# Two bursts of whole expert tiles in each of the last six iterations of the token pipeline, instead of all 71 tiles behind it

## What is computed

```python
x = x + conv_ref(group_norm(x), ...)      # depthwise 3x3, input-dependent weights, plus residual
t = tokens(x)
t = t + attn_ref(layer_norm(t), ...)      # hash buckets -> 32 pooled keys and values per image,
                                          # 8 heads of attention, then a GELU MLP 64 -> 256 -> 64
t = t + ffn_ref(layer_norm(t), ...)       # mixture of experts
# ffn_ref, for each token n, with 8 experts of hidden size 682 and the two likeliest chosen:
logits = flat @ router_w.T
topk_probs, topk_idx = top_k(softmax(logits), 2)
gates  = topk_probs / (sum(topk_probs) + 1e-9)
out[n] = sum over k of gates[k] * (silu(flat @ w1[e_k].T) * (flat @ w3[e_k].T)) @ w2[e_k].T
```

## Time and profile before

| | |
|---|---|
| median of 3 runs | 801.96 us (799.52 to 803.97) |
| profiled execution, its own time | 802.19 us |
| its span in the trace | 800.40 us |
| PE busy | 650.6 us, 81% of the span |
| DVE busy | 463.2 us, 58% |
| ACT busy | 353.7 us, 44% |
| POOL busy | 371.8 us, 46% |
| HBM read and written | 58.54 and 16.47 MB |

### The profile page before, as it was taken

The page is one execution under the profiler, slowest core; times in us unless marked ns, Lnnn a source line. Parts: engine busy times, 40 slices in busy tenths (PEclk is TensorE's granted clock), DMA queues, the critical chain, the costliest instruction groups (busy, mean ns, idle before and its releaser), DMA issues.

```text
span 800.4 us, 13968 instructions
## 1 busy us (share of the span) xinstructions
PE 650.6 (81%) x4632; PEld 487.2 (61%) x4632; DVE 463.2 (58%) x1094; ACT 353.7 (44%) x693; POOL 371.8 (46%) x377
## 2 busy tenths in 40 slices
PE   2597989797979797866206999999999999999960
PEld 2475858585857576664104777677777777777740
DVE  2356677686868676643502566655555665555545
ACT  1143646373727273533203555455555445555520
POOL 2204241767676768727670343334444333444440
PEclk9667868797978788575656999999999999999995
DMA  2000000010101010101173455555556455554608
GB/s 85 0 14 1 14 1 14 19 49 17 51 18 38 18 38 17 51 5 53 50 182 86 148 161 160 165 161 162 179 161 167 152 168 168 179 156 150 191 8 314
DMA packets 46615, 75.47 MB, mean 94 GB/s; under 512 B 7488, under 2 KB 30048, under 8 KB 46544
## 3 DMA queue, kind: packets, MB, share of 16 engines
q1 hardware_dynamic: 34512, 57.12, 24.5%
q0 software_dynamic: 8640, 12.74, 4.8%
q10 hardware_dynamic: 3392, 4.73, 1.8%
HBM read 58.54 MB, written 16.47 MB: 94 GB/s over the span
## 4 chain that ended last, share of the span: by engine, by line
PE 49%; POOL 23%; issue 17%; DVE 6%; DMA 3%; ACT 1%; POOLq 0%; SPq 0%; ACTq 0%; DVEq 0%
PE bk L757 25%; POOL expert_rows L497 15%; PE bk L768 12%; PE bk L745 3%; POOL rr L452 3%; PE bk L775 2%; POOL r L463 1%; PE bk L554 1%; POOL r L458 1%; POOL x2t L481 1%; DMA out<-hid 1%; DMA srow<-expert_results 1%; PE bk L642 1%; POOL grstd L441 1%; PE bk L616 1%
## 5 line engine op out<-in xcount | busy, mean ns | idle before, releaser
L1266 DVE TENSOR_TENSOR units<-bk,silu 128x512 f32<-128x512 f32 x213 | 147.3, 692 | 165.7 <-ACT silu L943 165.7
L519 POOL DMA_INDIRECT expert_results<-yout,xin x142 | 139.5, 983 | 218.3 <-DVE yout L1277 191.5
L757 PE MATMUL bk<-xs,wbuf 64*128 64x256 f32 x1704 | 205.5, 388 | 1.1 <-ACT xs L930 1.1
L757 PEld LDWEIGHTS bk<-xs,wbuf 64*128 64x128 f32 x1704 | 160.8, 189 | 44.4 <-issue 26.6
L943 ACT ACTIVATE silu<-bk 128x512 f32<-128x512 f32 x213 | 127.2, 597 | 87.2 <-PE bk L757 87.2
L497 POOL DMA_INDIRECT expert_rows<-srow,pos x128 | 132.4, 1034 | 44.2 <-issue 37.9
L768 PE MATMUL bk<-units,wbuf 128*64 128x256 f32 x852 | 107.6, 388 | 0.0
L768 PEld LDWEIGHTS bk<-units,wbuf 128*64 128x64 f32 x852 | 54.8, 136 | 32.4 <-issue 11.7
L935 ACT ACTIVATE ysb<-bk 128x256 f32<-128x256 f32 x71 | 27.2, 383 | 84.3 <-PE bk L768 84.3
L452 POOL TENSOR_TENSOR rr<-vare,c_mhalf 128x16 f32<-128x16 f32 x8 | 23.4, 2923 | 74.6 <-DVE vare L1046 74.6
L745 PE MATMUL bk<-const,xin 128*128 128x128 f32 x142 | 31.3, 302 | 29.2 <-DMA xin<-expert_rows 29.2
(11 more groups left out here) (184 smaller groups left out, 963.2 us busy)
## 6 DMA issues: line engine op xcount, KB each, us to landing
wbuf<-in_weights SPq DMA_DIRECT2D x71, 576.0 KB, 4.1
xin<-expert_rows SPq DMA_DIRECT2D x71, 130.0 KB, 2.4
expert_results<-yout,xin POOLq DMA_INDIRECT x142, 2.8
xg<-in_x SPq DMA_DIRECT2D x8, 256.0 KB, 2.8
expert_rows<-srow,pos POOLq DMA_INDIRECT x128, 2.4
srow<-expert_results SPq DMA_DIRECT2D x8, 256.0 KB, 5.1
srow<-expert_results ACTq DMA_DIRECT2D x8, 256.0 KB, 5.9
out<-hid ACTq DMA_DIRECT2D x8, 256.0 KB, 5.2
```

What stands on the lines that cost most here:

```text
L519: g.indirect_dma_start(results[:, :], bass.IndirectOffsetOnAxis(ap=xin[:, t % X_SLOTS, h, ROW - 1:ROW].bitcast(U32), axis=0), yout[:, t % ...
L757: last = mm(bank[:, ch * MT:(ch + 1) * MT], wbuf[part, t % W_SLOTS, at:at + P], xs[part, t % 2, :], start=True, stop=True)
L1266: tt(units[:, t % 2, q, :], h3_ps[q], silu[:, q, :], ALU.mult).then_inc(unit_ready, 1)
```

## The change

Iterations 0 to 4 (`ramp`) keep their lists. Iterations 5 to 10 (`mix`) have a new list on every engine, and in each of them PE runs two bursts of whole tiles, one ahead of the attention scores and one behind `fc2`. There is no iteration 11: the sixteen scatters of a group now all go out within its stage d. Because a tile may only take rows that are already scattered, tiles belong to rounds: iteration 5 has nine tiles, 6 to 9 have eight each, and iteration 10 has two in its first burst and the remaining 28 in its second. A tile of an early round must be full, which is known once the groups before have been counted; `schedule`, on DVE, works out each round's experts and rows from running counts. The router's product is now four matmuls with both halves of the tokens at once instead of eight, and the shifted scores and the probabilities (`ssub`, `prob`) have four buffers instead of two.

```diff
-ROW_SLOTS = 3
+ROW_SLOTS = 2
...
+MIX = 5
+FIRST_ROUND = 1
+ROUND_TILES = [0, 9, 8, 8, 8, 8, 8]
+MIXED = sum(ROUND_TILES)
...
+        def y_bank(t):
+            return (bk7, bk0)[(BURST_END[t] - 1 - t) % 2]
...
+def bursts():
+
+    table = {}
+    t = 0
+    for i in range(MIX, NG + 3):
+        n = ROUND_TILES[i - MIX + FIRST_ROUND]
+        half = 2 if i == NG + 2 else n // 2
+        last = i == NG + 2
+        table[i, 0] = (t, t + half)
+        table[i, 1] = (t + half, NT if last else t + n)
+        t += n
+    return table
```

SP loads three tiles ahead, weights and rows together (before: rows up to six ahead); the first rows of a round wait for that round's last scatter:

```diff
+            def load_tile(t):
+                if t < NT:
+                    load_weights(t)
+                    if t == MIXED:
+                        write_pads()
+                    load_rows(t)
+
+            def burst(i, part):
+                for t in range(*BURSTS[i, part]):
+                    load_tile(t + W_SLOTS - 1)
```

On POOL, the second burst has the scatters of rows and of results between each other:

```diff
+                run(d, row_destinations)
+                run(d, scatter, 0, 5)
+                if last:
+                    run(d, scatter, 5, 11)
+                else:
+                    run(c, rstd3)
...
+                if i == MIX:
+                    run(c, residual)
+                    run(d, rstd3)
+                    run(c, rstd2)
+                run(a, group_rstd)
...
+                def in_second(k):
+                    if k == 0:
+                        run(a, token_rstd)
+                        run(c, rstd3)
+                    if k == 1:
+                        run(b, rstd2)
+                    if i < NG + 2:
+                        run(d, scatter, 8 + 2 * k, 2 if k < 4 else 0)
+                    if k == 3:
+                        run(b, residual)
+                        run(a, token_sum)
+                        run(a, unit_sum)
+
+                burst(i, 0, in_first)
+                run(d, row_destinations)
+                run(d, scatter, 0, 8 if i < NG + 2 else 16)
+                burst(i, 1, in_second)
```

On PE:

```diff
+            def mixed_iteration(i, a=None, b=None, c=None, d=None):
+                if i == MIX:
+                    run(c, attend, 2)
+                    run(c, attend, 3)
+                    run(d, turn_wtok)
+                else:
+                    run(d, turn_wtok)
+                    turn_results(BURSTS[i - 1, 1][1] - 1)
+                    run(b, turn_n1, 0)
+                run(b, turn_n1, 1)
+                run(d, router)
+                run(b, rotate)
+                run(a, pair_means)
+                run(b, queries, 0)
+                run(c, turn_n2)
+                run(b, queries, 1)
+                run(a, pair_variances)
+                run(b, bucket_sums)
+                run(b, turn_pooled)
+                run(b, keys)
+                run(b, values)
+                turn_rows(BURSTS[i, 0][0])
+                burst(i, 0)
+                run(b, scores, 0)
+                turn_results(BURSTS[i, 0][1] - 1)
+                run(b, scores, 1)
+                run(a, convolution, 0)
+                run(b, scores, 2)
+                run(a, convolution, 1)
+                run(b, scores, 3)
+                run(d, places)
+                run(b, turn_prob, 0)
+                run(b, turn_prob, 1)
+                run(c, fc1, 0)
+                run(b, attend, 0)
+                run(b, attend, 1)
+                run(b, turn_prob, 2)
+                run(b, turn_prob, 3)
+                run(c, fc1, 1)
+                run(b, attend, 2)
+                run(b, attend, 3)
+                turn_rows(BURSTS[i, 1][0])
+                run(c, fc2)
+                burst(i, 1)
```

On ACT, what lies between the tiles of a burst (k is the tile's number in it):

```diff
+                def in_first(k):
+                    if k == 0:
+                        run(a, normalise_x)
+                    if k == 1:
+                        run(a, add_x)
+                        run(d, copy_rows)
+
+                def in_second(k):
+                    if k == 0:
+                        run(c, squares3)
+                        run(a, squares1)
+                    if k == 1:
+                        run(b, squares2)
+
+                burst(i, 0, in_first)
+                run(b, exponentials, 0)
+                run(b, exponentials, 1)
+                run(b, exponentials, 2)
+                run(b, exponentials, 3)
+                run(b, store_prob, 0)
+                run(b, store_prob, 1)
+                run(a, store_tokens)
+                run(c, gelus, 0)
+                run(b, store_prob, 2)
+                run(b, store_prob, 3)
+                run(c, gelus, 1)
+                burst(i, 1, in_second)
```

On DVE:

```diff
+            def schedule(d):
+                if d < FIRST_ROUND:
+                    return
...
+                step_done(tt(over[:, :, :], wide(cnt8[:, :], nk),
+                             (k_rows if final else k_full).unsqueeze(1).broadcast_to([P, NE, nk]),
+                             ALU.is_gt if final else ALU.is_ge))
+                step_done(v.tensor_reduce(full[:, :], over[:, :, :], AX.X, ALU.add))
+                step_done(tt(tiles[:, :], full[:, :], done_tiles[:, 0:NE], ALU.subtract))
...
+                    step_done(tt(done_tiles[:, 0:NE], done_tiles[:, 0:NE], taken[:, :], ALU.subtract))
...
+            def burst(i, part, between):
+                first, end = BURSTS[i, part]
+                for t in range(first, end):
+                    for q in range(NU):
+                        gated(t, q)
+                    if t > first + 1:
+                        gate_out(t - 2)
+                    between(t - first)
+                gate_out(end - 2)
+                gate_out(end - 1)
...
+                def in_first(k):
+                    if k == 0:
+                        run(d, first_pick)
+                    if k == 1:
+                        run(d, second_pick)
+                    if k == 2:
+                        run(a, row_sums)
+
+                def in_second(k):
+                    if k == 0:
+                        run(a, variance1)
+                        run(b, centre2)
+                    if k == 1:
+                        run(c, variance3)
+                        run(a, normalise1)
+                        if i < NG + 2:
+                            run(d, schedule)
+                    if k == 2:
+                        run(b, variance2)
+                        run(c, normalise3)
+                        run(a, normalise0)
+                    if k == 3:
+                        run(b, normalise2)
+                        if i + 1 < NG:
+                            channel_statistics(i + 1)
+
+                burst(i, 0, in_first)
+                run(b, centre_scores, 0)
+                run(b, centre_scores, 1)
+                run(b, centre_scores, 2)
+                run(b, centre_scores, 3)
+                run(d, row_places)
+                if i == NG + 2:
+                    run(d, schedule)
+                run(a, centre1)
+                run(b, attended, 0)
+                run(b, attended, 1)
+                run(c, centre3)
+                burst(i, 1, in_second)
```

More of the change, by code:

```diff
@@ L499, in scatter, with scatter_results @@
                         srow[:, d % ROW_SLOTS, k, j, :], None).then_inc(scattered[d % ROW_SLOTS], 16)
[L501 to L515 removed]
+            def scatter_results(t):
                 pool.wait_ge(yout_ready, t + 1)
@@ new lines, in turn_results, with burst @@
+            def turn_results(t):
+                pe.wait_ge(ysb_ready, t + 1)
+                for h in range(2):
+                    last = turn(y_bank(t)[:, MT + h * P:MT + (h + 1) * P], ysb[:, t % 2, h * P:(h + 1) * P], ident)
+                last.then_inc(y_turned, 1)
+            def burst(i, part):
+                first, end = BURSTS[i, part]
+                for t in range(first, end):
+                    for q in range(NU):
+                        up(t, q)
+                    if t + 1 < end:
+                        turn_rows(t + 1)
+                    if t > first + 1:
+                        turn_results(t - 2)
+                    if t > first:
+                        down(t - 1)
+                turn_results(end - 2)
+                down(end - 1)
@@ L948, in _, with silus, burst @@
-            store_results(NT - 1)
+                f(ysb[:, t % 2, :], y_bank(t)[:, 0:MT], ACT.Copy).then_inc(ysb_ready, 1)
+            def silus(t, q):
+                n = NU * t + q
+                act.wait_ge(h1_ready, n + 1)
+                wait(act, unit_ready, n - NU + 1)
+                f(silu[:, q, :], h1_ps[q], ACT.Silu).then_inc(silu_ready, 1)
+            def burst(i, part, between):
+                first, end = BURSTS[i, part]
+                store_xs(first)
+                for t in range(first, end):
+                    for q in range(NU):
+                        silus(t, q)
+                    if t + 1 < end:
+                        store_xs(t + 1)
+                    if t > first:
+                        store_results(t - 1)
+                    between(t - first)
+                store_results(end - 1)
```

(11 more changed lines are left out.)

575 lines of the change are left out of this document (333 added, 242 removed).

## The result

The changed kernel takes 841.94 us (median of 4 runs, 839.47 to 842.74) against 800.92 us of the kernel before in the same comparison: ratio 1.050, 95% interval 1.046 to 1.054. Forecast were 810 us and 768 to 832, so the sign was right and the size was not, and the time lies outside the range. The profiled execution took 841.85 us, its span is 840.0 us.

The account below looks back on a forecast made before the run. Pipeline bound by a chain through POOL's scatters and pows, tiles by PE. First burst at 228, rest of iteration 5 73.3, iterations 6 and 7 178, 8 to 10 302.5, tail 27.1: 808.9, about 810 us; range 768 to 832.

Parts of the forecast that it names:

- an iteration of 89 us: Full mixed iteration with eight tiles: head 20.5, first burst 23.0, middle 21.0, second burst 24.5 us; 79.5 before.
- The start: Iteration 5: eleven more scatters ahead of rstd3 delay the turn of wtok to near 208, 15 us lost once.
- The first bursts: Four tiles ahead of the attention scores: 23.0 us, with a slow first tile; 21.5 at full clock.
- The middle: PE from scores to fc2, between the two bursts: 21.0 us, with hardly a hole.
- The second bursts: Four tiles behind fc2: 24.5 us, set by DVE's 22.9 us of work against PE's 19.3.
- The tail: From the last w2 product's end to the end of the span: 27.1 us, as before.
- The step that failed: First tiles of bursts: the sum had no term for waiting for rows, and took the last scatters and padding rows as covered.
- The third rival: POOL's pows and next round's rows come late, second burst at half clock: 5 us an iteration, 832; chance 0.13.
- the half clock at the start of the head: Head of a mixed iteration, turn_wtok to values: TensorE at half clock, 20.5 us; 15.5 at 2.4 GHz.
- The rival that TensorE keeps 2.4 GHz: Full clock through head and first tile: iteration 81.5 us, sum 783; chance 0.25.
- The burst bound by PE alone: Bursts: DVE's additions find room and the holes close; iteration 72 us, sum near 742; chance 0.10.
- The rule on SBUF ports: Second burst: normalise1 might wait for rstd3's pow, up to 2 us an iteration, kernel near 818; left out of the sum.

Follow-up runs that it names:

- experiment 3: The eleven extra scatters of iteration 4 on POOL moved behind the pows of rstd3 and rstd2, against the changed kernel; 835.0 us.
- experiments 4 and 7: 4: constant turns in the holes of TensorE's heads, against the changed kernel, 836.7 us; 7: kernel 7, the same turns added to four order edits, 776.0 us.
- kernel 10: Changed kernel with four order edits, constant turns, statistics in the middle, new start, POOL's sums in the next iteration's first burst; 762.5 us.
- experiments 8 and 9: 8: kernel 7 with POOL's sums, statistics and start moved, 774.0 us; 9: as 8, sums in the next iteration's first burst and rstd2 earlier, 765.6 us.
- experiments 1 and 2: Each against the changed kernel. 1: more row scatters ahead of the second burst, 809.2 us; 2: padding rows written two tiles earlier, 832.0 us.
- kernel 7: Changed kernel with row scatters first, padding rows earlier, start scatters behind the pows, schedule in the middle, and constant turns in the heads; 776.0 us.

## Why the prediction was right in sign, by luck, and wrong in size

**Right in sign, by luck.** The forecast's 1% came from an iteration of 89 us that was thought to lose 9.5. Its pieces other than the waits measured 12 us less than the sum had, and with them alone the kernel would have been even with the one before. What made it slower was a term that stood at nothing.

**Right.** The start: turn_wtok at 207.6 for 208, first `up` at 227.3 for 228 (though a third of the 13.8 us lost had a second cause, experiment 3). The first bursts, 22.6 to 24.1 us for 23.0. The middle, 20.7 for 21.0 in iterations 5 to 7. The second bursts of iterations 6 and 7, 23.6 for 24.5, with the hole behind schedule (2.08 us for 2.5, schedule itself 3.8 us long for the 3.9 worked out from the earlier trace rows) and the one at the end (1.0 to 1.1 for 1.5) where I had put them. The tail, 27.5 for 27.1.

**The step that failed** is the one that gave the rows no term. The sum lets every first tile find its rows, on three grounds, and all three fail. First, that POOL "with some 53 us of work" in an iteration is not the bound: true of its busy time, but the row scatters are the last in its order, behind instructions that wait for DVE. Work and place are different questions, and I had asked only the first. Second, iterations 9 and 10 were sized by what TensorE does in them (62 us, and a head of 5), without asking what had covered the row loads in the heads of the fuller iterations. The rows are ready 15 to 18 us behind the burst's end ahead of each of iterations 7 to 10; a head of 13 us leaves 3 us of it, one of 4 us leaves 14. Third, "the last scatters (20 us) and the padding rows are covered by the six tiles left of round 6 (29 us)": each is shorter than the cover, but the padding rows stand behind another load on SP's queue and begin 21 us into the 27 that the six tiles take (661.8 to 689.1). Together 42.7 us; the other pieces, of which iterations 6 to 8 were forecast 3 to 5 us too long each, took back 12. The forecast's own last sign of being wrong, PE waiting for xin at the start of bursts, is what came.

The third rival, growing holes, named this mechanism ("the first rows of the next round ... come late") and was closest, at 832. Its price of 5 us in every iteration had the place wrong, and its second burst at half clock did not come: the products there take 2.86 us.

**The clock.** From the earlier trace rows I put the half clock at the start of the head. The rows of after show 1.00 there and 0.50 late in the head and in the first tile, and the head of iteration 6 took 17.7 us, not 20.5. The rival that TensorE keeps 2.4 GHz priced head and first tile at 7.5 us an iteration and 27 in all. A part of that was thus spared in the changed kernel already; for what was left experiments 4 and 7 measure 5.4 and 9.6 us in the whole kernel. So that rival could not have made the kernel faster by itself. The burst bound by PE alone (742) did not happen either, though kernel 10 has second bursts of 20.4 us for 19.3 of PE's work.

**The rule on SBUF ports.** The Trainium skill (SBUF — State Buffer, section Who interferes with whom) says that a DVE instruction with two SBUF inputs and a GpSimd instruction that reads SBUF exclude each other. I had weighed it for the pow of rstd3 against normalise1. There it did not show: normalise1 took 0.69 us, though it began 0.2 us ahead of the pow, and a centring with two SBUF inputs took 0.69 in the middle of a pow of 3.3 us (both in the changed kernel):

```profile
367.69 3.30 POOL L491 TENSOR_TENSOR rr<-vare,c_mhalf 128x16 f32<-128x16 f32 x1 [5.50 <-DVE vare L1269]
...
368.95 0.69 DVE L1257 SCALAR_TENSOR_TENSOR cent<-ssum,x 128x512 f32<-128x512 f32 x1
```

The prediction says that no row shows a pow against such an instruction. The trace of before did have one, a sum of u and att, both in SBUF, that took its 0.69 us in the middle of rstd3's pow:

```profile
351.75 1.67 POOL L463 TENSOR_TENSOR r<-vare,c_mhalf 128x8 f32<-128x8 f32 x1 [11.67 <-DVE vare L1140]
...
352.42 0.69 DVE L1113 TENSOR_TENSOR x<-u,att 128x512 f32<-128x512 f32 x1
```

For POOL's sums of 512 columns the trace agrees with it: 2.54 for 0.42 and 3.69 for 0.69, and both fall back when the sums go elsewhere (experiments 8 and 9). But "for as long as the first of them runs", as the prediction has it, is not what the rows show: wtok began at 356.68, 0.6 us ahead of the first sum, and ended at 360.37, behind the second, while the sums kept their 1.28 and 1.29 us.

## What to carry to other kernels

When work is interleaved, ask of each transfer three things: when its last producer stands in its engine's order (not how busy that engine is), which queue it stands in and behind what, and what covers it in the thinnest iteration, not in the typical one. A change that loses 5% can hide one that wins 5%: here the plan was sound, and some 42 us of the loss lay in the order of two helper engines (experiments 1 and 2). When the ends of runs scatter by 3 us, measure from an instruction that both kernels have alike.

## What was unexpected in the hardware

DVE instructions with two inputs in SBUF became many times as long beside POOL's sums of 512 columns (in kernel 7 one of 0.42 us took 3.11 at 452.68, one of 0.29 took 3.30 at 290.18, one of 0.16 took 2.68 at 372.70), and not at all beside POOL's pows of 8 and 16 columns, though these run longer (1.7 to 3.3 us). In iterations 6 to 8 the granted clock outlasted the holes at the end of a burst and fell only behind those late in the head; 25 short turns there, each about 0.15 us, kept it at 1.00 and made iteration 6's first tile 2.6 us shorter. What stays open: why the start of the common ramp scatters by 3.4 us between profiles, and how the last 3.4 us of waits for rows in iteration 10 of kernel 10 could go; neither was tried.
